# Attention of a macaron layer on one core: one key stack, other stores and side-work order, value products in two blocks

## The reference, cut to what matters

```
x = x + 0.5 * ffn(layernorm(x)); x = x + attn(layernorm(x)); x = x + 0.5 * ffn(layernorm(x))

def attn(x):                       # 16 sequences, S = 512, D = 128, 16 heads of 8
    q, k, v = (x @ W + b).reshape(B, S, 16, 8) for each of W = Wq, Wk, Wv
    scores = einsum('bthd,bshd->bhts', q, k) / sqrt(8) - slope[h] * |t - s|
    scores = where(s > t, -inf, scores)
    out = einsum('bhts,bshd->bthd', softmax(scores), v).reshape(B, S, 128)
    return out @ Wo + bo
```

## Time and profile before

| | before |
|---|---|
| median of 3 runs | 1024.37 us (1023.14 to 1026.57) |
| the profiled execution | 1028.07 us |
| its span, first to last instruction | 1026.4 us |
| granted TensorE clock, mean | 0.898 |
| busy in the span: TensorE, VectorE, ScalarE, GpSimd | 844.9, 746.9, 639.1, 537.0 us |
| DMA moved | 75.25 MB |

### The profile page before, as it was taken

How to read it: one execution, slowest core, us unless ns; L and a number is a source line. 1 busy time by engine, 2 the same in 40 slices (tenths; PEclk the granted TensorE clock), 3 DMA queues, 4 the chain that set the end, 5 groups by cost and what they waited for, 6 DMA issues and landing times. The chain is left out here.

```text
span 1026.4 us, 24158 instructions
## 1 busy us (share of the span) xinstructions
PE 844.9 (82%) x6498; PEld 397.3 (39%) x6498; DVE 746.9 (73%) x2534; ACT 639.1 (62%) x1538; POOL 537.0 (52%) x838
## 2 busy tenths in 40 slices
PE   4999996198898898799788878988987985999997
PEld 3444442043343343334334434433433423544443
DVE  4899995278686776767767866876866902899996
ACT  2767674106576676676666766776765773676765
POOL 3777775234364463553552643653643331677777
PEclk9999998557898898988988989989988997999999
DMA  6600000332322322322323223223223000011001
GB/s 164 99 0 0 0 0 1 106 124 96 137 77 87 137 78 91 121 95 92 108 87 113 96 86 126 87 87 134 84 83 134 13 1 21 12 31 31 23 29 42
DMA packets 61436, 75.25 MB, mean 73 GB/s; under 512 B 8084, under 2 KB 51988, under 8 KB 61204
## 3 DMA queue, kind: packets, MB, share of 16 engines
q1 hardware_dynamic: 61384, 74.61, 22.5%
HBM read 44.97 MB, written 29.36 MB: 72 GB/s over the span
## 5 line engine op out<-in xcount | busy, mean ns | idle before, releaser
L1104 DVE TENSOR_REDUCE att_neg_max<-att_max 128x1 bf16<-128x512 f32 (+3 forms) x704 | 411.5, 636 | 171.5 <-PE att_max L898 169.8
L997 ACT ACTIVATE att_probs<-att_exp 128x512 f32<-128x512 f32 x640 | 349.4, 598 | 188.3 <-PE att_exp L917 184.8
L1069 POOL TENSOR_SCALAR_AFFINE_SELECT att_probs<-att_probs 128x512 f32<-128x512 f32 x256 | 157.4, 637 | 316.8 <-ACT att_probs L997 316.8
L895 PE MATMUL att_max<-att_k_max,att_q_st 51*128 51x384 bf16 (+2 forms) x768 | 191.1, 300 | 99.3 <-DMA att_k_exp<-qk_parts 78.0
L917 PE MATMUL att_exp<-att_q_st,att_k_exp 64*128 64x512 bf16 (+3 forms) x1024 | 217.4, 321 | 4.0 <-DMA att_q_st<-att_shift 2.1
L933 PE MATMUL att_pv<-att_probs,att_v 128*32 128x512 f32 (+3 forms) x2048 | 207.2, 478 | 15.8 <-POOL att_probs L1069 15.8
L358 ACT ACTIVATE moe_scaled<-moe_hi,moe_gates 128x128 f32<-128x128 f32 x512 | 146.1, 372 | 61.2 <-PE moe_hi L304 60.9
L895 PEld LDWEIGHTS att_max<-att_k_max,att_q_st 51*128 51x128 bf16 x768 | 73.8, 98 | 281.6 <-DVE att_neg_max L1104 148.4
L898 PE MATMUL att_max<-att_k_max,att_q_st 62*128 62x128 bf16 x1024 | 178.2, 231 | 0.0
L518 DVE SCALAR_TENSOR_TENSOR x<-moe_lo,moe_gates,x 128x128 f32 (+1 forms) x512 | 160.6, 338 | 20.1 <-PE moe_lo L298 18.9
L298 PE MATMUL moe_lo<-moe_we,moe_hT 128*128 128x512 f32 x256 | 136.0, 613 | 0.0
(11 more groups left out here) (81 smaller groups left out, 879.1 us busy)
## 6 DMA issues: line engine op xcount, KB each, us to landing
qk_parts<-att_parts SPq DMA_DIRECT2D x192, 128.0 KB
att_q_st<-qk_parts SPq DMA_DIRECT2D x64, 192.0 KB
att_k_max<-qk_parts SPq DMA_DIRECT2D x64, 192.0 KB
att_k_exp<-qk_parts SPq DMA_DIRECT2D x64, 192.0 KB
x<-in_L_attn_x SPq DMA_DIRECT2D x16, 256.0 KB, 2.9
out<-x SPq DMA_DIRECT2D x16, 256.0 KB, 2.3
moe_we<-in_L_ffn_We SPq DMA_DIRECT2D x2, 512.0 KB, 4.7
att_q_st<-att_shift SPq DMA_DIRECT2D x64, 4.0 KB, 2.1
```

Of the source, the lines that this page charges most:

```text
L895: nc.tensor.matmul(max_ps[m % RING][:, at:at + width - P], q_st[par][low:low + FINE_ROW, r, i * P:(i + 1) * P], k_max[par][low:low + FINE_ ...
L997: nc.scalar.activation(probs[g % 2][:, n, :], exp_ps[m % RING][:], ACT.Exp).then_inc(exp_done, 1)
L1069: nc.gpsimd.affine_select(out=view, in_=view, compare_op=ALU.is_ge, fill=0.0, base=0, pattern=[[0, 4], [1, P]], channel_multiplier=-1).the ...
L1104: nc.vector.tensor_reduce(neg_max[par][:, g // 2, 1 - g % 2, heads[0]:heads[0] + len(heads), i], max_ps[m % RING][:, 0:len(heads) * width] ...
```

## The change

One key stack `k_st` takes the place of `k_max` and `k_exp`. Its rows are 48 of parts, 3 of bias, far, shift, then the fine rows. The max scores of the diagonal tile use all 64 rows, so the shift row of `q_st` must be zero there: each `stack` first writes zeros into it (`no_shift`, 8 KB). The exponentials use the first 53 rows. A part of q or k is stored once for all terms that use it, by one DMA with a repeating source (3, 2 and 1 terms), after the columns of Wq and Wk have been reordered on the host so that a partition maps to one row of the scratch. A shift is placed by one DMA in place of two. The side work, the splits and the layer norm move to earlier units, turn_h by a sequence, and the value products of a group run as two blocks, j = 0 and 1 after unit 5, j = 2 and 3 after unit 9.

```diff
-K_PARTS = [0, 1, 2, 0, 1, 0]
+K_PARTS = [1, 0, 2, 0, 1, 0]
+PART_TERMS = [[slice(0, 3), slice(3, 5), slice(5, 6)], [slice(1, 6, 2), slice(0, 5, 4), slice(2, 3)]]
-FINE_ROW = ALIBI_ROW + 3
+FAR_ROW = ALIBI_ROW + 3
+SHIFT_ROW = FAR_ROW + 1
+FINE_ROW = SHIFT_ROW + 1
-FAR_ROW = FINE_ROW + FINES
-SHIFT_ROW = FAR_ROW + 1
-assert SHIFT_ROW + 1 == SIDE
+assert FINE_ROW + FINES == SIDE
...
+        rows[SHIFT_ROW - ALIBI_ROW] = 0
+        self.no_shift = nc.inline_tensor(np.zeros((2, PAIRS // 2, S), np.uint16), "no_shift").ap().bitcast(BF16)
...
-    {3: "turn_h", 7: "project_q"},
-    {0: "project_k", 5: "shift_hi", 9: "turn_o1"},
-    {3: "turn_o", 7: "shift_lo"},
-    {0: "project_v", 4: "output", 9: "turn_o0"},
+    {2: "project_q", 4: "shift_hi", 8: "project_k"},
+    {1: "turn_o1", 6: "project_v"},
+    {1: "turn_o", 6: "shift_lo", 10: "output"},
+    {1: "turn_o0", 8: "turn_h"},
-PREPARE = {(0, 10): "split_q0", (1, 0): "split_q1", (1, 1): "split_q2", (1, 2): "split_q3",
-           (1, 3): "split_k0", (1, 4): "split_k1", (1, 5): "split_k2", (1, 6): "split_k3", (2, 4): "add_bias",
-           (3, 0): "statistics", (3, 1): "aggregate", (3, 2): "add_eps", (3, 3): "take_root", (3, 6): "shift_mean",
-           (3, 7): "normalise0", (3, 8): "normalise1", (3, 9): "normalise2", (3, 10): "normalise3"}
-PV_AFTER = {3: 0, 5: 1, 7: 2, 9: 3}
+PREPARE = {(0, 5): "split_q0", (0, 6): "split_q1", (0, 7): "split_q2", (0, 8): "split_q3",
+           (0, 10): "split_k0", (1, 0): "split_k1", (1, 1): "split_k2", (1, 2): "split_k3", (2, 5): "add_bias"}
+NORMALISE = {(2, 0): "statistics", (2, 1): "aggregate", (2, 2): "add_eps", (2, 3): "take_root", (2, 7): "shift_mean",
+             (2, 8): "normalise0", (2, 9): "normalise1", (2, 10): "normalise2", (3, 0): "normalise3"}
+PV_AFTER = {5: (0, 1), 9: (2, 3)}
...
-        SCRATCH_DMAS = len(Q_PARTS)
-        STACK_DMAS = 6
-        SHIFT_DMAS = 2
+        SCRATCH_DMAS = 3
+        STACK_DMAS = 5
+        SHIFT_DMAS = 1
...
-            offset = {"turn_h": 2, "project_q": 2, "project_k": 2, "project_v": 1, "shift_lo": 1, "shift_hi": 0,
+            offset = {"turn_h": 3, "project_q": 2, "project_k": 2, "project_v": 1, "shift_lo": 1, "shift_hi": 0,
...
-                    if on_prepare and (g, n) in PREPARE:
-                        if g < GROUPS - 1 and there(b + 2):
-                            on_prepare(b + 2, par, half + 1, PREPARE[g, n])
-                        if g == GROUPS - 1 and there(b + 3):
-                            on_prepare(b + 3, 1 - par, half + par + 1, PREPARE[g, n])
+                    if on_prepare and (g, n) in PREPARE and there(b + 2):
+                        on_prepare(b + 2, par, half + 1, PREPARE[g, n])
+                    if on_prepare and (g, n) in NORMALISE and there(b + 3):
+                        on_prepare(b + 3, 1 - par, half + par + 1, NORMALISE[g, n])
-                        if g > 0 and there(b):
-                            on_pv(b, par, g - 1, PV_AFTER[n])
-                        if g == 0 and there(b - 1):
-                            on_pv(b - 1, 1 - par, GROUPS - 1, PV_AFTER[n])
+                        for j in PV_AFTER[n]:
+                            if g > 0 and there(b):
+                                on_pv(b, par, g - 1, j)
+                            if g == 0 and there(b - 1):
+                                on_pv(b - 1, 1 - par, GROUPS - 1, j)
...
         def _(sp):
             def store_parts(b, par, half, side):
-                which = (Q_PARTS, K_PARTS)[side]
-                for term in sorted(range(len(which)), key=lambda t: which[t]):
-                    part = which[term]
+                for part, terms in enumerate(PART_TERMS[side]):
-                    sp.dma_start(scratch[par, side, term].rearrange("u d r s -> r (u d) s"),
-                                 parts[side][:, part]).then_inc(scratch_in[par][side], DMA)
+                    dst = scratch[par, side, terms].rearrange("t u d r s -> (u d r) t s")
+                    sp.dma_start(dst, parts[side][:, part].unsqueeze(1).to_broadcast(list(dst.shape))).then_inc(
+                        scratch_in[par][side], DMA)
             def stack(b, par, half, hf):
-                if hf == 0:
-                    for side in range(2):
-                        sp.wait_ge(scratch_in[par][side], half * (SCRATCH_DMAS * DMA) + SCRATCH_DMAS * DMA)
+                pairs = slice(hf * PAIRS // 2, (hf + 1) * PAIRS // 2)
-                pairs = slice(hf * PAIRS // 2, (hf + 1) * PAIRS // 2)
-                for side, stacks in ((0, (q_st,)), (1, (k_max, k_exp))):
-                    for dst in stacks:
-                        for ab in range(2):
-                            sp.dma_start(dst[par][ab * SIDE:ab * SIDE + HEAD_ROWS, pairs, :],
-                                         scratch[par, side, :, ab, :, pairs]).then_inc(
-                                stack_in[par][hf], DMA)
+                sp.dma_start(q_st[par][SHIFT_ROW:SHIFT_ROW + SIDE + 1:SIDE, pairs, :],
+                             consts.no_shift).then_inc(stack_in[par][hf], DMA)
+                for side, dst in enumerate((q_st[par], k_st[par])):
+                    if hf == 0:
+                        sp.wait_ge(scratch_in[par][side], half * (SCRATCH_DMAS * DMA) + SCRATCH_DMAS * DMA)
+                    for ab in range(2):
+                        sp.dma_start(dst[ab * SIDE:ab * SIDE + HEAD_ROWS, pairs, :],
+                                     scratch[par, side, :, ab, :, pairs]).then_inc(stack_in[par][hf], DMA)
             def place_shift(b, par, half, hf):
-                for ab in range(2):
-                    rows = PAIRS // 2 * T
-                    sp.dma_start(q_st[par][ab * SIDE + SHIFT_ROW:ab * SIDE + SHIFT_ROW + 1, pairs, :],
-                                 shift[ab * rows:(ab + 1) * rows, :]).then_inc(shift_in[par][hf], DMA)
+                sp.dma_start(q_st[par][SHIFT_ROW:SHIFT_ROW + SIDE + 1:SIDE, pairs, :],
+                             shift[:]).then_inc(shift_in[par][hf], DMA)
             def step(b, par, half):
...
-                                         q_st[par][low:low + FINE_ROW, r, i * P:(i + 1) * P],
-                                         k_max[par][low:low + FINE_ROW, r, 0:width - P], start=True, stop=True)
+                                         q_st[par][low:low + FAR_ROW, r, i * P:(i + 1) * P],
+                                         k_st[par][low:low + FAR_ROW, r, 0:width - P], start=True, stop=True)
-                                          q_st[par][low:low + FAR_ROW, r, i * P:(i + 1) * P],
-                                          k_max[par][low:low + FAR_ROW, r, width - P:width], start=True, stop=True)
+                                          q_st[par][low:low + SIDE, r, i * P:(i + 1) * P],
+                                          k_st[par][low:low + SIDE, r, width - P:width], start=True, stop=True)
...
-                                          k_exp[par][low:low + SIDE, r, j * P:(j + 1) * P],
-                                          q_st[par][low:low + SIDE, r, j * P:S], start=True, stop=True)
+                                          k_st[par][low:low + FINE_ROW, r, j * P:(j + 1) * P],
+                                          q_st[par][low:low + FINE_ROW, r, j * P:S], start=True, stop=True)
...
-                    nc.scalar.activation(hT[par][:], side_ps[:], ACT.Copy).then_inc(side_read, 1)
+                    nc.scalar.activation(hT[1 - par][:], side_ps[:], ACT.Copy).then_inc(side_read, 1)
...
     arrays = {f"in_{n}": np.ascontiguousarray(inputs[n]) for n in _INS}
+    for n in ("Wq", "bq", "Wk", "bk"):
+        a = arrays[f"in_L0_attn_{n}"]
+        by_side = a.reshape(-1, PAIRS, 2, HD).transpose(0, 2, 3, 1)
+        arrays[f"in_L0_attn_{n}"] = np.ascontiguousarray(by_side).reshape(a.shape)
```

More of the change, by code:

```diff
@@ L110, in __init__ @@
         q_far = 2.0 ** np.round(-0.43 * (np.arange(S) - S // 2) - 15)
-        self.k_max_rows, self.k_exp_rows = [], []
+        fine_at, far_at = FINE_ROW - ALIBI_ROW, FAR_ROW - ALIBI_ROW
+        self.k_rows = []
         for ab in range(2):
@@ L114, in __init__ @@
             rows[0:3] = bf16_parts(slopes[ab::2, None] * np.arange(S)[None, :], 3)
+            rows[far_at] = bf16_parts(k_far, 1)[0]
             rows[SHIFT_ROW - ALIBI_ROW] = one
[L116 to L123, removed]
+            rows[fine_at:] = bf16_parts(k_fine, 1)[0][:, None]
+            self.k_rows.append(nc.inline_tensor(rows, f"k_rows_{ab}").ap().bitcast(BF16))
+        rows = np.full((SIDE - ALIBI_ROW, PAIRS, S), one, np.uint16)
+        rows[far_at] = bf16_parts(q_far, 1)[0]
+        rows[SHIFT_ROW - ALIBI_ROW] = 0
+        rows[fine_at:] = bf16_parts(q_fine, 1)[0][:, None]
         self.q_rows = nc.inline_tensor(rows, "q_rows").ap().bitcast(BF16)
+        self.no_shift = nc.inline_tensor(np.zeros((2, PAIRS // 2, S), np.uint16), "no_shift").ap().bitcast(BF16)
 def moe_layer(nc, tag, x, consts, Wr, We, x_in=None, out=None, ahead=None):
@@ L614, in __init__ @@
```

(17 more changed lines are left out.)

## The result

The changed kernel takes **988.4 us** (median of 4, 985.5 to 989.6) against 1023.8 in the same session: ratio 0.965, 95% interval 0.961 to 0.969. It is faster, as forecast, but by 35 us and not by 94; the forecast of 930 and its range of 898 to 978 missed it.

What follows compares the result with a forecast made beforehand. No engine filled the 39.6 us attention step; late stack loads, the slow clock after them and masks held TensorE. Steps of 33.5 us save 79, edges 15: 1028.1 becomes 934, less 3.7 is 930 us, range 898 to 978.

Steps and rivals of the forecast that it cites:

- The chain: Shift, stores and key stack in SyncE's queue: first store at about 5 us of a step, half stack issued by 19.
- Stall: TensorE's wait for a late stack load in nearly each attention step: 3.8 us a step would leave.
- mask wait: TensorE's wait for a mask in group 2 of a step: 0.95 us goes, group 2 passed about 1.1 us earlier.
- The rival with fewer engines: Repeating-source stores run on 3 or 2 DMA engines, 6.5 us each, so the kernel gets slower, 1057 us; chance 0.05.
- The edges: First load, step 0, step 14 and tail, outside the 13 steady steps: 15 us saved together, bounds 8 and 20.
- 0.45 us idle, four times a step, 1.8 us: VectorE runs dry behind each double value block, its ring of three max tiles covering 1.75 us.
- +1.9 us out of -1 to +5: Net cost a step of double blocks and side-work pairs less saved switching, added to 31.6 us.
- The clock: Rival: TensorE's slow clock stays in every step, losing 3.1 us a step, 970 us; chance 0.04.
- The switching saved: Eight fewer value block entries and exits on TensorE at 0.4 us each: 3.2 us a step saved.
- 31.6 us without any of these terms: Attention step after removing stall, slow clock and mask wait: 39.6 - 3.8 - 3.1 - 1.1 us.
- side work: Three side-work pieces one unit from a value block, VectorE idle 1.2 us each: 3.6 us a step as upper bound.
- starved readers: Rival: VectorE and ScalarE idle in each of TensorE's long blocks, 36.6 to 37 us a step, 976 us; chance 0.12.

Runs made afterwards that it cites:

- DMA part: Changed kernel's single key stack, six stores and one shift DMA, with the earlier kernel's places for side work, splits and layer norm, four value blocks: 945.6 us, ratio 0.922.
- placement: Side work, splits and layer norm at their new places, with the earlier kernel's two key stacks, twelve stores and two shift DMAs, four value blocks: 941.2 us, ratio 0.919.
- late-pair run: Changed kernel with j = 0 after unit 3, j = 1 after unit 5, and j = 2 and 3 as one block after unit 9: 923.3 us, ratio 0.899.
- four blocks: Changed kernel with the value products in separate blocks again, after units 3, 5, 7 and 9, all else as changed: 933.1 us, ratio 0.912.
- the run with less layer norm work: Changed kernel, its attention layer norm taking statistics of one tile of four from the second sequence on (result not the reference's): 963.1 us, ratio 0.938.

## Why the prediction was wrong, point by point

**The chain: right.** Stall gone, mask wait gone, first store after 5.5 us (forecast 5), the last by 15.4 (15), at 171 GB/s in that stretch (over 157), half stack at 16.8 (16 to 19). The experiments add what the sum did not say: DMA part and placement are each enough. The rival with fewer engines falls by this row of the changed kernel's page, a 384 KB store landed after 2.7 us (6.5 us by that rival):

```profile
qk_parts<-att_parts SPq DMA_DIRECT2D x32, 384.0 KB, 2.7
```

The Trainium skill, "DMA: Bandwidth & Descriptors", section "Why a DMA increments its semaphore by 16 and not by 1", gives the rule by which the prediction had put the new stores on 16 engines. The row agrees with it, though it doesn't count engines.

**The edges: 9 us and not 15.** The first max matmul comes at 195.4 and not at 206.6 us, 11 us earlier where 7 were taken. But step 0 takes 37.0 us, hardly less than before, where 4 us were to be saved, and from the start of step 14 to the end the kernel takes 2 us more (238.3 against 236.2), where 4 less were forecast.

**The term that failed** is "0.45 us idle, four times a step, 1.8 us", with the choice of +1.9 us out of -1 to +5 built on it. The early double block leaves VectorE idle for 5.7 us a step. Its length was right: from the weight load at 484.43 to the next one, 1.64 us.

```profile
484.43 0.16 PEld L924 LDWEIGHTS att_pv<-att_probs,att_v 128*32 128x32 f32 x8 [0.21 <-issue]
...
486.07 0.09 PEld L886 LDWEIGHTS att_max<-att_k_st,att_q_st 51*128 51x128 bf16 x1 [0.62 <-DVE att_neg_max L1095]
```

What was wrong is the backlog set against it. I took a full ring, 1.75 us. VectorE finished its last reduction at 483.28 + 2.21 = 485.49, so it had 1.06 us of work when the block began: the ring holds three units at the moment unit 5 may be issued, but one of them is read while the unit's own scores and the switch pass, and the two that are left are narrow ones (in the changed kernel a reduction of 384 columns took 0.55 us on average and one of 512 took 0.68, so 1.1 us for the two). 1.64 + 0.38 until the next product - 1.06 = 0.96 us, the 0.95 measured. The row of 1.21 us idle behind a stretch of 1.62 us showed that size, and I used it only for side work.

**The clock** was a rival of its own with 0.04. It came in ten of the 13 steps, mostly once and in group 2. Against the 35.9 us of a step without, those ten are together about 19 us longer. It was argued away with groups 1 to 3 of the kernel before, but the statistics had moved next to a block that had become long. In the late-pair run, with the same statistics and the block short, no steady step had a dip. The Trainium skill, "TensorE: Matmul & The Clock Gate", section "A second HAM failure mode: psum-queue depth-cycling", spoke for this rival: frequent short idle times of TensorE between groups of matmuls, as it cycles through PSUM, make the clock swing. The windows above agree, with no idle time between TensorE's matmuls over 1 us in the stretch before the fall.

**The switching saved** was set at 3.2 us for eight entries. The late merges, four entries fewer, measured 33.7 - 33.0 = 0.7 us, all their effects together.

Set against the prediction's 31.6 us without any of these terms, a step with four blocks took 33.7: side work and all else cost 2.1 us, where the sum had 3.6 as the upper bound. The early merge then added 4.5 us and the late one took off 0.7, +3.8 us for the two, where the sum had 1.8 - 3.2 = -1.4.

In sum, the 13 steps took 483.2 us, 37.2 each (the six of the window above 37.5), outside the bound of 36.6. That is 3.7 us a step over the forecast, 48 of the 58 us by which it missed. The edges are 6 more, and 5 come from the way from the profiled execution to the median: 3.7 us were taken off, but the median lay 1.1 above the profiled 987.3. The rival "starved readers" had the mechanism, the sign and nearly the number (976 us). The nearness is in part luck: its 36.6 to 37 us a step came from the upper bound, in which the side-work pairs stood with 3.6 us and the double blocks with 1.8, and it had no clock.

The best kernel is the changed one with only the late pair merged: 923.3 us, 65 under the changed one, at a ratio of 0.899 to the kernel before.

## What to carry to other kernels

Before merging blocks on an engine that feeds others through a ring, take the consumer's unfinished work at the block's first instruction, read from the timeline, not the ring's depth times the mean. In the one block worked out above, what was longer came back as idle time to within 0.01 us, and the shorter late pair even gained. Such a cost can hide behind a larger stall: here the same two merges cost 0 us with the stall and 55 without. Keep work of the consumer's own, such as statistics, away from the longest block, since the producer's clock can fall between them.

## What the runs showed of the hardware

TensorE's clock fell from 1.00 to 0.50 after a stretch in which it was busy for 2.11 of 3.40 us, with no idle time over 1 us and no wait for a DMA, so a DMA stall is not needed for it; at equal work a step with the dip took 1.5 to 1.7 us more (changed kernel, and the run with less layer norm work). Six stores with a source that repeats 3, 2 or 1 times left in 4.3 us (DMA part alone) where twelve plain ones of the same bytes took 8.1 in the kernel before; a 384 KB one landed after 2.7 us.
